# Fused attention and mixture of experts on one core: VectorE exponentiates four head tiles of a key block instead of three

## What is computed

```
xn  = layernorm(x)                                   # (4, 1024, 128)
q, k, v = heads(xn @ Wq.T), heads(xn @ Wk.T), heads(xn @ Wv.T)   # 16 heads of 8 channels
q, k = rope(q), rope(k)
attn = softmax(q k^T * 8**-0.5) v                    # full 1024 x 1024 scores for each head
gate = softmax(xn @ gate_w + gate_b);  vals, idx = top_k(gate, 2)
ffn  = sum over the 2 chosen of 8 experts of vals * (gelu(gelu(xn w1 + b1) w2 + b2) w3 + b3)
out  = x + attn + ffn
```

## Time and profile before

| what | value |
|---|---|
| median of the runs | 632.62 us |
| span of the profiled execution, first to last instruction | 630.1 us |
| TensorE matmul busy | 597.7 us (95%) |
| ScalarE busy | 536.9 us (85%) |
| VectorE busy | 338.4 us (54%) |
| GpSimd busy | 195.7 us (31%) |
| late steps 9 to 15 | 427.9 to 630.1 us of the span |

### The profile page before, as it was taken

The page is one execution under the profiler, slowest core; times in us unless marked ns, Lnnn a source line. Parts: engine busy times, 40 slices in busy tenths (PEclk is TensorE's granted clock), DMA queues, the critical chain, the costliest instruction groups (busy, mean ns, idle before and its releaser), DMA issues.

```text
span 630.1 us, 12248 instructions
## 1 busy us (share of the span) xinstructions
PE 597.7 (95%) x4152; PEld 259.9 (41%) x4152; DVE 338.4 (54%) x819; ACT 536.9 (85%) x548; POOL 195.7 (31%) x187
## 2 busy tenths in 40 slices
PE   9889999999999999998999999999999999999996
PEld 6323333232322222222799999993222222222221
DVE  5654233785343335121555555555494958668475
ACT  3799999999999999999554555559999999999995
POOL 2700000000554444441121222223645648484000
PEclk9999999999999999999999999999999999999999
DMA  8653711523363446693433333310312122121311
GB/s 230 172 196 136 264 36 35 217 101 119 127 218 124 146 147 211 211 302 67 105 81 71 79 75 75 75 44 22 104 36 87 48 69 63 58 84 57 113 44 35
DMA packets 82621, 70.67 MB, mean 112 GB/s; under 512 B 44288, under 2 KB 58400, under 8 KB 82576
## 3 DMA queue, kind: packets, MB, share of 16 engines
q1 hardware_dynamic: 76000, 56.34, 29.5%
q0 software_dynamic: 5856, 13.05, 6.8%
q10 hardware_dynamic: 720, 0.71, 0.5%
HBM read 32.92 MB, written 32.96 MB: 105 GB/s over the span
## 4 chain that ended last, share of the span: by engine, by line
PE 64%; ACT 16%; issue 10%; DVE 5%; DMA 2%; ACTq 0%; SPq 0%; DVEq 0%
PE ps L1496 13%; PE ps L1430 10%; ACT probs L731 9%; PE ps L1480 8%; PE ps L1553 6%; PE ps L1422 5%; PE ps L1443 5%; ACT probs L696 4%; PE ps L1526 4%; PE ps L1403 4%; PE ps L1347 2%; ACT probs L674 2%; DMA k_st<-k_d 2%; PE ps L1383 2%; PE ps L1310 1%
## 5 line engine op out<-in xcount | busy, mean ns | idle before, releaser
L696 ACT ACTIVATE probs<-ps 128x1536 f32<-128x1536 f32 (+1 forms) x154 | 206.1, 1426 | 6.7 <-PE ps L1480 6.3
L731 ACT ACTIVATE probs<-ps 128x1536 f32<-128x1536 f32 x140 | 190.2, 1520 | 2.0 <-PE ps L1526 1.9
L574 POOL DMA_INDIRECT slots_x_d<-xn_all,slot_i x64 | 62.5, 977 | 195.7 <-DVE expert_i L1037 127.2
L1496 PE MATMUL ps<-probs,v_st 128*32 128x512 f32 x896 | 119.5, 604 | 1.3 <-DVE v_st L839 0.7
L710 ACT ACTIVATE work<-ps,work 128x256 f32<-128x256 f32 (+1 forms) x156 | 64.9, 454 | 60.5 <-PE ps L1430 60.2
L1553 PE MATMUL ps<-probs,v_st 128*32 128x512 f32 x840 | 111.5, 604 | 0.5 <-DVE o_sb L922 0.5
L612 POOL DMA_INDIRECT work<-slots_y_d,slot_i x64 | 89.8, 1404 | 64.6 <-PE ps L1553 48.4
L1480 PE MATMUL ps<-q_st,k_st 32*128 32x512 f32 x448 | 77.2, 494 | 6.8 <-ACT probs L696 3.7
L1526 PE MATMUL ps<-q_st,k_st 32*128 32x512 f32 x420 | 71.1, 494 | 8.8 <-ACT probs L731 8.7
L1480 PEld LDWEIGHTS ps<-q_st,k_st 32*128 32x128 f32 x448 | 28.9, 181 | 114.6 <-ACT probs L696 80.0
L1526 PEld LDWEIGHTS ps<-q_st,k_st 32*128 32x128 f32 x420 | 26.4, 181 | 108.0 <-ACT probs L731 99.0
(11 more groups left out here) (193 smaller groups left out, 564.3 us busy)
## 6 DMA issues: line engine op xcount, KB each, us to landing
k_d<-parts SPq DMA_DIRECT2D x8, 1024.0 KB, 5.3
q_d<-parts SPq DMA_DIRECT2D x8, 1024.0 KB, 6.1
q_st<-q_d SPq DMA_DIRECT2D x30, 256.0 KB, 3.3
k_st<-k_d SPq DMA_DIRECT2D x30, 256.0 KB, 3.2
slots_x_d<-parts SPq DMA_DIRECT2D x5, 1024.0 KB, 7.5
work<-slots_x_d SPq DMA_DIRECT2D x128, 32.0 KB, 1.9
slots_y_d<-work POOLq DMA_DIRECT2D x32, 128.0 KB, 2.2
work<-work SPq DMA_DIRECT2D x24, 128.0 KB, 2.1
```

Source lines behind the costliest of these rows:

```text
L696: nc.scalar.activation(group_probs(phase, g)[:, 0:size, :], group_slot(g)[:, 0:size * HALF].rearrange("p (h n) -> p h n", n=HALF), ACT.Exp ...
L731: nc.scalar.activation(late_probs(g), group_slot(g).rearrange("p (h n) -> p h n", n=HALF), ACT.Exp, scale=SCALE).then_inc(S["exp_done"], 1)
L1496: ins = nc.tensor.matmul(o_ps[32 * h:32 * h + 32, :], v_window(mt, h, half), group_probs(phase, half * HALF_GROUPS + g)[:, n, :], start=(j ...
```

## The change

In steps 9 to 14 the help block is block 0 of the first query half, its scores are made at groups 1 to 4, and VectorE reads and exponentiates all four tiles, with the same eight instructions at 128x2048. ScalarE exponentiates none of them. The last step, 15, keeps the old way (block 0 of the second half, groups 2 to 5, three tiles on VectorE and one on ScalarE). The intermediate `he_t` is gone, and `he_p` is the place of the help block's probabilities itself. `gath` has two buffers, used in turn, so that GpSimd waits only for the additions of two steps before. The additions are moved: those of the first expert stand two by two behind the first three reads, those of the second behind `normalise`. The first of them still waits for all gathers of the step before. The output's transposes at g = 9 wait for the four reads of the help tiles and no longer for ScalarE's tile.

```diff
-HELP_AT = 2
-HELP_HEADS = (0, 3, 2, 1)
+def help_at(last):
+    return 2 if last else 1
...
-        gath = part(0, 2 * GATHER * C).rearrange("p (k c) -> p k c", c=C)
-        he_s, he_t, he_g, he_p = (part(2 * GATHER * C + 3 * HALF * k, 3 * HALF) for k in range(4))
+        gath = part(0, 4 * GATHER * C).rearrange("p (a k c) -> p a k c", a=2, c=C)
+        he_s, he_g = (part(4 * GATHER * C + HG * HALF * k, HG * HALF) for k in range(2))
...
+        he_p = help_probs.rearrange("p h n -> p (h n)")
...
-                if i >= 1:
-                    pool.wait_ge(S["combined"], i)
+                if i >= 2:
+                    pool.wait_ge(S["combined"], i - 1)
...
-                    if g == HELP_AT + 5:
+                    if last and g == help_at(last) + 5:
                         act.wait_ge(S["help_scored"], (t - SPLIT) * HG + HG)
                         nc.scalar.activation(help_probs[:, 0, :], aux_ps, ACT.Exp, scale=SCALE).then_inc(S["help_exp"], 1)
...
+            def combine(i, c, lo=0, hi=GATHER):
+                end = min(GATHER * i + GATHER, TILES)
+                if lo == 0:
+                    dve.wait_ge(S["comb_chain" if c else "gathered"], end if c else 32 * end)
+                for tile in range(GATHER * i + lo, min(GATHER * i + hi, end)):
...
-            def read_help(t):
-                for k in range(3):
+            def read_help(t, tiles):
+                for k in range(tiles):
...
-                    if t > SPLIT and k < 2:
-                        combine(t - SPLIT - 1, k)
+                    if t > SPLIT and k < 3:
+                        combine(t - SPLIT - 1, 0, 2 * k, 2 * k + 2)
...
-                help_exps(t)
+                help_exps(t, HG)
                 if t > SPLIT:
                     normalise(t - 1)
+                    combine(t - SPLIT - 1, 1)
...
-                    if HELP_AT <= g < HELP_AT + HG:
-                        help_scores(t, g - HELP_AT)
-                    if g == HELP_AT + 7 and not first:
-                        turn(t - 1, 0, True)
+                    if help_at(last) <= g < help_at(last) + HG:
+                        help_scores(t, g - help_at(last), last)
+                    if g == 9 and not first:
+                        turn(t - 1, 0, "last" if last else "late")
```

More of the change, by code:

```diff
@@ L97, in blocks_full, with help_head, help_place @@
     return g // HALF_GROUPS * MT + heads_of(g)[-1][0] + 1
-LATE_ITEMS = [(0, mt, h) for mt in range(MT) for h in range(HG)] + [(1, mt, h) for mt in range(1, MT) for h in range(HG)]
+LATE_BLOCKS = [(0, mt) for mt in range(1, MT)] + [(1, mt) for mt in range(MT)]
+LAST_BLOCKS = [(0, mt) for mt in range(1, MT)] + [(0, 0)] + [(1, mt) for mt in range(1, MT)]
+LATE_ITEMS, LAST_ITEMS = ([(half, mt, h) for half, mt in blocks for h in range(HG)] for blocks in (LATE_BLOCKS, LAST_BLOCKS))
 LATE_GROUPS = len(LATE_ITEMS) // 3
-LATE_BLOCKS = [(0, mt) for mt in range(MT)] + [(1, mt) for mt in range(1, MT)]
-HELP_AT = 2
-HELP_HEADS = (0, 3, 2, 1)
 HELP_VALUES = 17
+def help_at(last):
+    return 2 if last else 1
+def help_head(k, last=False):
+    return (0 - k - help_at(last) - 2) % HG
+def help_place(h, last=False):
+    k = [help_head(k, last) for k in range(HG)].index(h)
+    return (k + 1) % HG if last else k
 EXP_COEFFS = (-7.287735462188721, 41.80864715576172, -180.93753051757812, 522.0867309570312, -753.2122192382812)
@@ L719, in _, with late_exps @@
             nc.scalar.activation(fb[:, 3:4], zeros[:, 0:1], ACT.Exp)
-            def late_exps(t, first=False):
+            def late_exps(t, first=False, last=False):
                 for g in range(LATE_GROUPS):
@@ L737, in _ @@
             late_exps(SPLIT, True)
-            with act.Fori(SPLIT + 1, STEPS) as t:
+            with act.Fori(SPLIT + 1, STEPS - 1) as t:
                 late_exps(t)
+            late_exps(STEPS - 1, last=True)
             act.wait_ge(S["flag_made"], 1)
@@ L1171, in _ @@
             finish_y(CYCLES, 0)
[L1173 to L1182, removed]
+            def combine(i, c, lo=0, hi=GATHER):
[3 more added lines that the diff above has]
+                for tile in range(GATHER * i + lo, min(GATHER * i + hi, end)):
+                    ins = nc.vector.scalar_tensor_tensor(x_all[:, tile, :], gath[:, i % 2, GATHER * c + tile - GATHER * i, :], gates[:, tile, c:c + 1],
+                                                         x_all[:, tile, :], ALU.mult, ALU.add)
+                    if c == 0:
+                        ins.then_inc(S["comb_chain"], 1)
+                    elif tile == end - 1:
+                        ins.then_inc(S["combined"], 1)
             def finish_rows(tile, tiles):
@@ L1237, in _ @@
             last = STEPS - 1
-            read_help(last)
-            help_exps(last, 0, 4)
+            read_help(last, HG - 1)
+            combine(last - SPLIT - 1, 1)
+            help_exps(last, HG - 1, 0, 4)
             normalise(last - 1)
             copy_o(last, 0)
-            help_exps(last, 4)
+            help_exps(last, HG - 1, 4)
             normalise(last, (0,))
@@ L1405, in values, with turn @@
                 ins.then_inc(S["pv_done"], 1)
-            def turn(t, half=0, helped=False):
-                if helped:
-                    pe.wait_ge(S["help_exp"], t - (SPLIT - 2))
+            def turn(t, half=0, helped=None):
+                if helped == "late":
+                    pe.wait_ge(S["help_read"], (t - (SPLIT - 2)) * HG)
+                elif helped == "last":
+                    pe.wait_ge(S["help_exp"], 1)
                 free_aux(aux_of_turn(t, half))
@@ L1513, in step, with late_scores @@
                         group_values(t - 1, BLOCKS - 1, 1 - phase)
-            def late_scores(t, g, first=False):
-                items = LATE_ITEMS[3 * g:3 * g + 3]
+            def late_scores(t, g, first=False, last=False):
+                items = (LAST_ITEMS if last else LATE_ITEMS)[3 * g:3 * g + 3]
                 if g == 0:
@@ L1522, in late_scores @@
                     pe.wait_ge(S["kb_loaded"], t * 16 + 16)
+                if not last and (1, 0, 0) in items:
+                    pe.wait_ge(S["q1_loaded"], t * 16 + 16)
                 if g >= 2 or not first:
@@ L1529, in late_scores, with help_scores @@
                 ins.then_inc(S["scores_done"], 1)
[L1531 removed]
+            def help_scores(t, k, last=False):
                 if k == 0:
[L1534 removed]
+                    if last:
+                        pe.wait_ge(S["q1_loaded"], t * 16 + 16)
                     free_aux(aux_of_turn(t - 1))
                 else:
[L1537 to L1539 removed]
+                    pe.wait_ge(S["help_read"], (t - SPLIT) * HG + k)
+                h = help_head(k, last)
+                cols = slice(HALF, N) if last else slice(0, HALF)
+                nc.tensor.matmul(aux_ps, k_st[32 * h:32 * h + ROWS, 0:P], q_st[32 * h:32 * h + ROWS, cols],
                                  start=True, stop=True).then_inc(S["help_scored"], 1)
             def late_values(t, n, apart=False):
[L1544 removed]
+                half, mt = (LAST_BLOCKS if apart else LATE_BLOCKS)[n]
                 pe.wait_ge(S["exp_done"], group_units(t) + ((HG * n + HG - 1) // 3 + 1))
[L1546 to L1547 removed]
+                if (half, mt) in ((0, 1), (0, MT // 2)):
+                    pe.wait_ge(S["v_loaded"], t * 2 + (1 if mt == 1 else 2))
                 begins, ends = (n in (0, MT), n in (MT - 1, len(LATE_BLOCKS) - 1)) if apart else (n == 0, n == len(LATE_BLOCKS) - 1)
@@ L1567, in late_step @@
                     if g < LATE_GROUPS - 1:
-                        late_scores(t, g + 1, first=(first and g == 0))
+                        late_scores(t, g + 1, first=(first and g == 0), last=last)
                     elif not last:
@@ L1582, in late_step @@
                     if g == HELP_VALUES:
-                        help_values(t)
+                        help_values(t, last)
                     if g > 0:
```

28 lines of the change are left out of this document (15 added, 13 removed).

## The result

The changed kernel takes 646.17 us in the median of five runs (643.48 to 647.0), the kernel before 632.62, by now also the median of five. The ratio is 1.0207, with a 95% interval of 1.0194 to 1.0219. The forecast was slower, 641.5 us, in a range that ended at 644.5, so the measured time lies above it. The direction and the place were as forecast. The size was not: +13.5 us against +8.9.

The account below looks back on a forecast made before the run. ScalarE was taken as the bound, with one stall and TensorE close behind. Late gathers lengthen steps: 0.2 (step 9) + 0.85 (10) + 1.5 (11) + 6.3 (three more) = +8.9 on 632.62, 641.5 us; range 635.5 to 644.5.

Parts of the forecast that it names:

- one stall of 0.5: ScalarE's late step: a hole of 0.40 that costs 0.52 us, staying after the change with another cause.
- ScalarE's gain and the reads: Late steps: six ScalarE help tiles go, at most 2.9 us; the second help tile waits for the first read.
- the chain's end: VectorE's help exponentials end at 507.4 in step 11's clock, leaving some 0.25 of the 0.48 us gain.
- VectorE's chain: Eight help-exponential instructions on VectorE: 2.29 and 1.23 us each by kind, 16.45 us in all against 12.7.
- The gathers: GpSimd's twelve gathers a step: last start 22.8 us after the first, landing 2.2 later, so VectorE stands 2.6 us.
- The hold to an instruction's end: A gather starting under a long two-input VectorE instruction is held to its end, then needs 0.82 us.
- the closed loop's sum: From first gather through landing, additions, reads and values to the next first gather: 30.0 us against 27.90, +2.1 a step.
- the second rival: The same as Half the holding: 637.0 us, chance 0.13.
- the way from the last start to the first addition: Within a step's loop, from the last gather's start: landing 2.2 us and wake 0.05.
- Half the holding: GpSimd's gathers held under VectorE's chain but not by small additions or final sum: +4.3, 637.0 us, chance 0.13.
- The faster rival: GpSimd's gathers keep their 1.79 us pace and land before the first read ends: 631.2 us, chance 0.11.
- No change: Gathers keep their pace, but VectorE's chain at 2.35 us an instruction takes the whole gain: 632.6 us, chance 0.08.

Follow-up runs that it names:

- e5: e1 with VectorE exponentiating three help tiles in all steps and ScalarE the fourth again: 633.53 us, ratio 1.0009 to the kernel before.
- e6: e1 with the help tiles of steps 10 to 14 made earlier, the first at group 19 of the step before: 629.38 us, ratio 0.9940.
- e1: Changed kernel with all twelve additions behind the normalisation in steps 10 to 14, gathers counted on two semaphores: 631.36 us, ratio 0.9981 to the kernel before.
- e3: Changed kernel with each pair of gathers allowed three value blocks earlier, counted on two semaphores: 631.47 us, ratio 0.9997 to the kernel before.
- e2: Changed kernel with two matmuls of zeros in TensorE's wait before the third help tile, steps 10 to 14: 639.64 us, ratio 1.0124 to the kernel before.

## Why the prediction was right in its direction and wrong in its size

**What bounds the kernel.** ScalarE with 26.8 us a step, one stall of 0.5 and the help tile's 0.48. Borne out: e5, which has all three, makes steps of 27.9, and e6, which has neither the tile nor most of the stall, goes down to 26.9.

**ScalarE's gain and the reads.** I let the first read's place behind the copy eat what the stall had cost, and the chain's end eat half of the 0.48, for steps of 27.65. e1 and e3, which have both and no late gather, make 27.55 to 27.6 from step 11 on. Right. The 0.3 us a step between e5 and e1 is the 0.25 of the sum.

**VectorE's chain.** 2.29 and 1.23 us were taken for the two kinds of instruction, and both were measured as that. The upper end of 2.35 was too high by its own rate: 1.76 + 512 x 1.09 ns = 2.32.

**The gathers.** The hold to an instruction's end, 0.82 us behind it, was right, to 0.01 us. So was the count of seven gathers under the chain's eight instructions, where the clock held (e1, e2). One of them is held over two instructions, the long one that it meets and the TENSOR_SCALAR of 1.23 us behind it: 2.59 us in e2. The last start was put 21.6 to 22.7 us behind the first in step 10 and 22.8 in the steps after it; 22.0, 22.4, 22.0 and 22.0 were measured. But the last part of that was wrong. I let the final sum hold a gather and allowed for a hold by the additions, and neither was seen: the gather from 514.86, under the additions, took 0.94. In the kernel before, a gather that started under the final sum was held, and in e1 one is again (1.41). Here, in step 11, one started at 516.11, just ahead of the final sum at 516.27, and took 0.95. Why additions of 128x128 don't hold, though they read two tensors as the long ones do, no run tells.

**The step that failed: the closed loop's sum.** It counted the way from the second read to the next first gather at full speed: 0.43 + 1.0 + 0.43 + 1.87 = 3.73 us behind the third help tile. In step 14, at clock 1.00, that way took 3.7 us, from the help tile at 586.99 to the gather at 590.71. In step 12 it took 6.05 us, from 524.86 to 530.91, with the values at 1.94 us and the clock at 0.50. That is 2.3 us more. From the third help tile to the first gather, steps 10, 11 and 13 took 4.73, 5.26 and 4.57 us, so 5.7 us were missing over the five steps, which fits the 5.3 to 6.5 that e2 gives back. The prediction prices TensorE's work at full clock everywhere, without a reason for it; in the page of before the granted clock is 9 in all slices. But the change itself, by my own account, put a wait of some 2 us into TensorE. A term for what that does to the clock belonged in the sum, or at least a rival with its price, since a value block takes 1.94 us at half clock and 1.07 at full clock. With it the loop would have been up to 30.0 + 2.3 = 32.3 us. Measured between the first gathers of two steps, it was 31.0, 32.2, 30.4 and 29.4. The slower clock also delays the first gather against VectorE's chain, so that it meets a later instruction: in step 11 it took 3.56 us, and 1.05 in e2, where the clock held.

**The size without the clock.** e2 says 639.6, the sum said 641.5. So at full clock the sum was 1.9 us too high, and the truth lay between it and the second rival, at 637.0. The steps of e2 are 29.1 us where the sum had 30.0. Its gathers last 21.6 us from first to last start, as in that rival, and not 22.8. Against that, the way from the last start to the first addition was put at 2.25 us and took 2.57 in e2's step 11 and 2.48 in the changed kernel's step 12. Steps 9 and 10 were put 0.9 us too short together.

**The rivals.** Half the holding had the gathers right in their last part, but lacked the clock as well, and its time was further off. The faster rival rested on 1.49 being the gather's own time. It fell with 2.02 in the changed kernel and 1.49 in e5. No change, by the chain's upper end, fell with 2.29 us an instruction and e1's steps of 27.6. None of the rivals had a term for the clock. The Trainium skill's inference in SBUF — State Buffer, "Who interferes with whom", that a two-input instruction leaves descriptor generation alone, disagrees with these 2.02 us for this indirect DMA. The rule that it stands beside, that such an instruction takes the read interface from a GpSimd operation that reads SBUF, agrees with them, but does not tell why the additions of 128x128 held none.

## What to carry to other kernels

Before making an engine's instructions longer, look for what another engine does only between them: here a gather that needs 0.94 us was held to the end of the long VectorE instruction that it met, so instructions 30% longer put the gathers 30% further apart, on an engine that looked 69% idle. A wait belongs in an in-order queue behind everything that others wait for. Moving 1.7 us of additions turned +2.1% into -0.2%, with nothing else changed but the semaphores that count the gathers. And when a sum puts a new wait into TensorE, the work behind it is to be priced at both clock levels.

## What the runs showed that I had not expected

The waits ahead of the half clock were short. In step 11 TensorE stood for 0.36 and then 0.79 us between blocks, and the values behind took 1.93 us:

```profile
490.69 0.49 PE L1569 MATMUL ps<-q_st,k_st 32*128 32x512 f32 x1 [0.36 <-DVE work L1217]
491.11 1.07 PE L1583 MATMUL ps<-probs,v_st 128*32 128x512 f32 x8
...
493.41 0.49 PE L1569 MATMUL ps<-q_st,k_st 32*128 32x512 f32 x1 [0.79 <-DVE work L1217]
493.83 1.93 PE L1583 MATMUL ps<-probs,v_st 128*32 128x512 f32 x8
```

In step 14 it stood for 1.09 us at the same place, and the clock stayed at 1.00:

```profile
586.99 0.49 PE L1569 MATMUL ps<-q_st,k_st 32*128 32x512 f32 x1 [1.09 <-DVE work L1217]
587.41 1.06 PE L1583 MATMUL ps<-probs,v_st 128*32 128x512 f32 x8
```

In step 10 the waits were 0.41 and 1.06 us and the clock fell at once. In step 13 they were 0.37 and 1.25, the first block of values still took 1.07 us, and the next took 1.92. So the lengths of these waits don't tell whether and when the clock falls. That may also be why the five runs of the changed kernel spread over 3.5 us, the fastest of them with the highest mean clock, 0.991. It isn't shown: the kernel before, which spread over 1.1 us in the runs beside them, spread over 5.0 in 25 later ones.
